# Hardware loops in place of unrolled code, over most of a transformer layer kernel

## The reference

```python
x = x + xattn(layernorm(x), ctx, ...)     # 16 heads of 16, rope on q and k, softmax over 256
x = x + gla(layernorm(x), ...)            # scan over 64 tokens, 16 heads, 8 keys by 16 values
x = x + moe(layernorm(x), ...)            # silu(x @ wg) * (x @ wu) @ wd, hidden size 704
```

## Time and profile before

| | us |
|---|---|
| median of 3 runs | 2263.97 (2263.96 to 2264.1) |
| the profiled execution | 2263.97 |
| its span, first to last instruction | 2262.1 |
| TensorE / VectorE / ScalarE busy | 1827.0 / 1470.0 / 1100.3 |
| GpSimd busy | 746.7 |

### The profile page before, as it was taken

How to read it: one execution, slowest core, us unless ns; L and a number is a source line. 1 busy time by engine, 2 the same in 40 slices (tenths; PEclk the granted TensorE clock), 3 DMA queues, 4 the chain that set the end, 5 groups by cost and what they waited for, 6 DMA issues and landing times.

```text
span 2262.1 us, 52418 instructions
## 1 busy us (share of the span) xinstructions
PE 1827.0 (81%) x20028; PEld 1357.1 (60%) x20028; DVE 1470.0 (65%) x2810; ACT 1100.3 (49%) x2670; POOL 746.7 (33%) x849
## 2 busy tenths in 40 slices
PE   2777787777777777877777777658689999999998
PEld 1454555555555555555555555436578888888887
DVE  1687778878877787778788777747453333333347
ACT  1556555655566555556555655523353333333332
POOL 2343333333424332433334343207212323232320
PEclk8888888889889888889898898859899999999999
DMA  2100010000001000100010000012231111111133
GB/s 83 65 17 17 17 32 17 17 21 27 17 17 32 17 17 16 32 17 17 17 32 17 17 23 13 4 48 88 87 109 34 48 39 46 41 43 44 43 149 123
DMA packets 61455, 87.89 MB, mean 39 GB/s; under 512 B 7328, under 2 KB 49520, under 8 KB 61216
## 3 DMA queue, kind: packets, MB, share of 16 engines
q1 hardware_dynamic: 41232, 36.29, 5.3%
q0 software_dynamic: 10688, 33.11, 4.1%
q10 hardware_dynamic: 9296, 15.14, 2.1%
HBM read 66.16 MB, written 18.35 MB: 37 GB/s over the span
## 4 chain that ended last, share of the span: by engine, by line
PE 57%; DVE 23%; issue 9%; ACT 6%; POOL 3%; SPq 1%; DMA 1%; ACTq 0%; DVEq 0%; POOLq 0%
PE ps L1022 16%; PE ps L708 12%; PE ps L1035 9%; PE ps L716 8%; PE ps L703 7%; DVE experts L1430 3%; POOL experts L653 3%; DVE experts L1440 2%; DVE work L1412 2%; ACT experts L1152 2%; DVE experts L1456 2%; PE ps L785 1%; PE ps L846 1%; ACT work L1112 1%; DVE experts L1490 1%
## 5 line engine op out<-in xcount | busy, mean ns | idle before, releaser
L1022 PE MATMUL ps<-work,experts 128*128 128x256 f16 x3888 | 443.9, 276 | 17.6 <-ACT work L1317 8.9
L1022 PEld LDWEIGHTS ps<-work,experts 128*128 (+1 forms) x3888 | 380.8, 99 | 68.5 <-issue 10.4
L703 PE MATMUL ps<-cst,experts 128*128 128x128 f32 x1376 | 238.9, 313 | 124.9 <-DVE experts L1490 56.8
L1112 ACT ACTIVATE experts<-ps 128x512 f16<-128x512 f32 (+3 forms) x416 | 253.7, 647 | 81.0 <-PE ps L703 74.3
L703 PEld LDWEIGHTS ps<-cst,experts 128*128 128x128 f32 x1376 | 177.3, 160 | 176.0 <-issue 111.1
L708 PE MATMUL ps<-experts 128*128 128x512 f32 (+1 forms) x640 | 281.5, 580 | 1.4 <-ACT experts L1112 1.4
L1112 ACT ACTIVATE work<-work 128x768 f16<-128x768 f32 x108 | 90.9, 842 | 364.3 <-PE ps L1035 225.5
L1171 ACT ACTIVATE experts<-ps,experts 128x256 f32<-128x256 f32 x512 | 235.7, 476 | 64.4 <-DVE experts L1430 64.4
L1035 PE MATMUL ps<-experts,work 128*128 (+3 forms) x1944 | 237.8, 273 | 2.9 <-DVE work L1705 2.9
L582 POOL TENSOR_TENSOR experts<-experts,cst 128x128 f32<-128x128 f32 x256 | 135.1, 564 | 288.7 <-DVE experts L1440 288.7
L1697 DVE SCALAR_TENSOR_TENSOR work<-ps,work 128x768 f32<-128x768 f32 x108 | 103.4, 957 | 166.5 <-PE ps L1022 164.8
(11 more groups left out here) (187 smaller groups left out, 3042.1 us busy)
## 6 DMA issues: line engine op xcount, KB each, us to landing
experts<-in_ctx SPq DMA_DIRECT2D x32, 512.0 KB, 4.6
experts<-choice_out POOLq DMA_DIRECT2D x8, 1024.0 KB, 13.2
experts<-in_x SPq DMA_DIRECT2D x32, 128.0 KB, 2.2
token_in<-experts SPq DMA_DIRECT2D x32, 128.0 KB, 1.7
work<-token_in SPq DMA_DIRECT2D x32, 128.0 KB, 2.3
work<-in_L_ffn_routed_gate ACTq DMA_DIRECT2D x8, 352.0 KB, 3.1
work<-in_L_ffn_routed_up ACTq DMA_DIRECT2D x8, 352.0 KB, 4.0
out<-x_all POOLq DMA_DIRECT2D x5, 512.0 KB, 3.3
```

Source lines behind the costliest of these rows:

```text
L703: ins = pe.transpose(bank[:, k * P:(k + 1) * P], a, ident)
L1022: ins = pe.matmul(ps[:, 1 + 3 * part + c // 2, (c % 2) * R:(c % 2 + 1) * R], experts_h[:, e, at:at + P], e_rows_t[k][:, b * DK + kk, :], s ...
L1112: nc.scalar.activation(dst, src, ACT.Copy).then_inc(done, 1)
```

## The change

Part of each Python loop becomes a loop that the hardware runs (`Fori`): the body stands once in the program, a register holds i, and a compare and branch at its end goes back to its head.

- The attention steps 3 to 30 on GpSimd, TensorE, ScalarE and VectorE: 14 turns of two steps. On SyncE, steps 3 to 28: 13 turns.
- TensorE's tiles 4 to 7: two turns of two tiles. Its tiles 10 to 45: 18 turns of two. At the head of such a turn three expert numbers are read (that of the tile before, and those of the two tiles), where before each tile read its own.
- ScalarE's tiles 10 to 51: 21 turns of two. VectorE's tiles 12 to 47: 36 turns of one.

In a loop the wait values and the addresses that depend on the step or tile are computed from i by register instructions. The order of the work on each engine stays.

```diff
@@ over_pairs @@
-        for k in range(3, NPAIR - 1):
-            body(Step(0, k))
+        with eng.Fori(1, (NPAIR - 2) // 2) as i:
+            body(Step(i, 1))
+            body(Step(i, 2))
@@ sync @@
-        for k in range(3, NPAIR - 3):
-            step(Step(0, k))
+        with sp.Fori(1, (NPAIR - 4) // 2) as i:
+            step(Step(i, 1))
+            step(Step(i, 2))
@@ tensor @@
-        for t in range(TABLE, FIRST - 1):
-            tile(t, t % 2, 0, 0)
+        with pe.Fori(TABLE // 2, FIRST // 2 - 1) as i:
+            tile(i * 2, 0, 0, 0)
+            tile(i * 2 + 1, 1, 0, 0)
+        tile(FIRST - 2, 0, 0, 0)
         tile(FIRST - 1, 1, 0, 0, True)
         pe.wait_ge(S["chunk_lo_ready"], NCHUNK * NE)
-        def expert_of(t):
-            return pe.value_load(tile_e[0:1, t:t + 1], min_val=0, max_val=NE)
-
-        e_before = 0
-        for t in range(FIRST, MID):
-            e = expert_of(t)
-            if t + 1 < MID:
-                tile(t, t % 2, e, e_before, True)
-            else:
-                last_tile(t, e, e_before)
-            e_before = e
-        last_tile(MID, 0, e_before)
+        with pe.Fori(FIRST // 2, MID // 2 - 1) as i:
+            e = [pe.value_load(tile_e[0:1, bass.ds(i * 2 + m, 1)], min_val=0, max_val=NE) for m in range(-1, 2)]
+            tile(i * 2, 0, e[1], e[0], True)
+            tile(i * 2 + 1, 1, e[2], e[1], True)
+        e = [pe.value_load(tile_e[0:1, MID - 3 + m:MID - 2 + m], min_val=0, max_val=NE) for m in range(3)]
+        tile(MID - 2, 0, e[1], e[0], True)
+        last_tile(MID - 1, e[2], e[1])
+        last_tile(MID, 0, e[2])
@@ scalar @@
-        for t in range(FIRST, NT - 1):
-            tile(t, t % 2)
+        with act.Fori(FIRST // 2, NT // 2 - 1) as i:
+            tile(i * 2, 0)
+            tile(i * 2 + 1, 1)
+        tile(NT - 2, 0)
@@ vector @@
-        for t in range(FIRST + 1, MID):
+        slot_tile(FIRST + 1)
+        with dve.Fori(FIRST + 2, MID) as t:
             slot_tile(t)
```

## The result

The changed kernel takes 2329.35 us (median of 4, 2328.55 to 2330.69) against 2264.03 us (2263.96 to 2267.43): a ratio of 1.0285, 95% interval 1.0268 to 1.0303, slower by 65 us. Its profiled execution took 2326.99 us with a span of 2325.2, so 63.1 us more span than before. The forecast was +22; the direction and the range held, the size did not.

What follows compares the result with a forecast made beforehand. Attention was taken to be bound by a chain through the engines, the tiles by TensorE alone. Terms of 11.6 + 4.2 + 3.9 + 2.6 = 22.3 us on 2263.97 gave 2286.3 us; range 2258 to 2340.

Steps and rivals of the forecast that it cites:

- What bounds each part: Attention steps are limited by a chain passing from engine to engine, the tiles by TensorE alone.
- Register values and indices: Attention steps: wait values from i at nine chain places, 11.6 us; indices of `x2_all` and `logits`, 4.2 us.
- "hidden" rival: Sequencers are ahead everywhere that matters, so all four terms vanish: 2264 us, no change; chance 0.2.
- Back edges of the attention loops: At 13 turn ends the branch hides in gaps; late-read waits ahead of the scores cost 0.3 us each, 3.9 us.
- The rival of the fetched head: Loop heads must be loaded again at back edges: 2347 to 2411 us, or 2312 to 2338 if only attention; chance 0.25.
- Tile heads: TensorE's routed tiles, 17 back edges: a 1.76 us head just inside 1.9 us of cover, 0.15 us each, 2.6 us.
- ScalarE, VectorE, SyncE and GpSimd at nothing: ScalarE's and VectorE's tile loops and the work of SyncE and GpSimd have time to spare and cost nothing.
- the third rival: Attention steps: the two-step rhythm removes TensorE's lower-clock steps, gaining up to 13 us, 2251 us; chance 0.1.

Runs made afterwards that it cites:

- Experiment 1: The changed kernel with TensorE's three loops as straight code again; 2314.83 us, ratio 0.9992, on a chip where the kernel before takes 2316.95 us.
- experiment 12: The changed kernel with a branch prefetch hint on TensorE's attention loop and the expert-number reads spread over the turn; 2264.98 us, ratio 1.0006.
- Experiment 7: The changed kernel with expert numbers read where they are needed, not all at the head of a routed-tile turn; 2309.49 us, ratio 1.02.
- slot 0: The changed kernel with the head of TensorE's attention loop at the first slot of a 256-instruction block; 2312.84 us, ratio 1.0225.
- the kernels of four and six tiles: The kernel before with only TensorE's routed tiles 10 to 45 looped, four or six a turn; 2298.61 us (1.015) and 2315.33 us (1.0224).

## Why the prediction was wrong

**What bounds each part: right.** Attention is a chain through the engines, so the late scores moved every step behind them; the tiles wait for TensorE's own sequencer alone, and that is what happened to them.

**Register values and indices, 11.6 + 4.2 us: too high, measured near nothing.** Experiment 1 has all of them but TensorE's and takes 0.9992 of the time; experiment 12 has all of them and takes 1.0006, and its interval ends at 1.0014, 3 us. Steps inside a turn take 44.1 us, no more than a step of before at a good clock. I had counted nine places of the chain at which a sequencer reads on only when its wait is met. Most likely the register instructions stand ahead of such a wait and are done while it lasts, though no run separates that. My "hidden" rival was right in this.

**Back edges of the attention loops, 3.9 us: the step that failed.** The prediction said that "each sequencer meets the branch early" and that TensorE had some 4 us from the new residual to the next scores. But TensorE's sequencer can't read ahead of a wait that isn't met. Its last waits of a step, ahead of the transposes and the logits, are met only as those start, so the branch begins at 1291.9, with 0.5 to 0.9 us of matmuls left in the queue at the 13 edges. ScalarE's and VectorE's branches come late as well, at 1293.4 and 1293.7, VectorE's 1.8 us behind the end of its last statistics and not at once; at 45 and 56 ns they cost nothing. The price of the branch was wrong as well: I bounded it by a self-standing wait, 51 ns, and a base, 151; it was 215 where the head is at hand and 3384 where it is not. 3.4 us on 13 edges are 44 us; half a microsecond an edge comes on top, some 10 us come back because steps take 44.1 us instead of 44.5, and 40.9 remain.

**The rival of the fetched head: right in the attention loop, wrong in the tiles.** I gave it 0.25 and priced an edge at 2 to 4 us, 2312 to 2338 if attention alone were hit. The time lies there, in part by luck: that sum holds 16 us for registers that did not come and 2.6 for tile heads that were 18.9. It was made from the packet size and a data load's 2.2 us, and I let the 4 us gaps argue it down, the same mistake as above. It should have been the likeliest: the body is seven packets long, and no row spoke for its head being kept. The rule of the Trainium skill (Runtime: NRT & Kernel Launch, Instruction fetch mechanics), that a taken branch out of the loaded window waits for a fetch, is borne out for the body of two steps: 3384 ns and nine packets an edge. The window that it names, two pages, is not: two packets hold 512 instructions, and TensorE's loops of 612 and 1218 kept their heads, with branches of 215 and 208 ns. So the tile loop lost nothing by a fetch, where the rival had put 35 to 73 us.

**Tile heads, 2.6 us: right mechanism, wrong size, 18.9 us.** The term weighed a head of 1.76 us against a cover of 1.9 us, and left 0.15 an edge. The cover was right, 2.0 us; the head takes 2.9. I had put a read and its base at 0.305 + 0.151 = 0.46 us; three reads in a row start 0.75 us apart, with entries and gaps between that the earlier trace rows showed only as separate groups. Three of them are 2.25, where I had 1.37. An edge costs 1.07 us, 17 edges 18.2. The prediction had priced the loss without cover at 22 us, and that is nearly what came. Experiment 7 confirms it: reads apart, no loss.

**ScalarE, VectorE, SyncE and GpSimd at nothing: right** (experiment 1).

**The clock: both ways.** In the regular rhythm the slower steps of before are gone, as the third rival said: every step without an edge takes 44.1 us instead of 44.5 on average. That they went because of the clock is likely and not shown: with the pauses gone, in experiment 12, the steps vary between 44.0 and 44.9 us again. The pauses cost several times what the rhythm gave.

The sum as it should have been: 0 + 0 + 41 + 19, and some 3 us between and behind the parts, 63 of span.

**What stays open.** Why a body of some 1800 instructions on TensorE keeps its head at some places in the program and at others not, and at slot 0 only at most edges; and how the hint works. With it, the packets were not fetched at another time but not at all. The 4.1 us between attention and tiles are explained in part. From the residual add of step 30 to the row transposes with which the routed tiles begin it is 265.7 us before, 269.7 after, 268.9 in experiment 12 and 267.0 in experiment 7. The last tile of this stretch holds the first turn's reads; it takes 18.0 to 19.6 us with one read (before, and experiments 7 and 12), and 20.3, 21.5 and 23.2 with three, five and seven (after, and the kernels of four and six tiles). Of the rest no run tells; experiment 12 makes it up in the attention steps.

## What to carry to other kernels

Before a long loop body is put on an engine, ask two things: whether its head will still be at hand when the branch comes back (the instruction queue's packets tell afterwards: the same number comes again for each edge if it is not), and what that engine has queued at that moment. A sequencer holding a wait is not ahead, however long its engine has been idle; cut the loop where matmuls are queued and the engine has time to spare behind them, or give a hint, and spread slow register reads over the body. If the straight code's fetching is hidden, a hardware loop at its best only makes the program shorter.

## What was not expected of the hardware

- A taken compare and branch whose target is at hand takes some 215 ns on TensorE, 56 on VectorE, 45 on ScalarE and GpSimd (medians). The Trainium skill (Advanced Engine Details and Errata, Control Flow Timing) gives some 108 ns; the runs here show values on both sides, by engine.
- A branch with a fetch of the head takes 3.3 to 3.9 us on TensorE, 4.5 and 4.8 at slot 0, against 2.2 us for a 128 KB load of data.
- A pause of 2.4 us in dense matmuls made a tile 2.6 or 4.3 us longer, depending on whether the granted clock was 1.00 or lower behind it (4.10 or 5.77 us for the same 36 matmuls).
- One chip runs the kernel before in 2317 us where the others take 2264. In the traces from it the routed tiles take some 14.15 us instead of 12.65, some 51 us over 35 tiles. A change that costs 19 us on one chip was so hidden on another.
